# Denominator and gate products with 128 columns in place of 16 and 8

## The chip, the cores and the metric

The kernel runs on one core of one Trainium2 chip. The metric is the device time of one execution in microseconds (us); smaller is better. The engines are named as in the profile: PE is TensorE's matrix product, PEld its loading of weights, DVE is VectorE, ACT is ScalarE, POOL is GpSimd, SP issues DMAs.

## What is computed

The input is x of shape (16, 512, 128): 16 sequences of 512 tokens, all in float32. The reference does, with the constants 16 heads of width 8:

```python
x = x + linear_attention(layernorm(x), W_in, W_out)
    # q, k, v = projections; q, k clipped; Chebyshev polynomials T0..T10 of both
    # num = sum_p beta_p * Tq_p * cumsum(Tk_p * v)      over the sequence
    # den = sum_p beta_p * sum(Tq_p) * cumsum(sum(Tk_p))  per head and token
    # out = (num / (den + 1e-7)) @ W_out.T
x = x + ffn(layernorm(x))
    # h = x + causal softmax attention(layernorm(x)), 16 heads
    # logits = layernorm(h) @ gate_W + gate_b; top 2 of 8 experts, softmax of the two
    # h + sum over the two experts of w_e * (gelu(layernorm(h) @ W1_e + b1_e) @ W2_e + b2_e)
```

The changed lines belong to the denominator `den` (one value for each of 16 heads and each token) and to the logits (one value for each of 8 experts and each token).

## The kernel before

One sequence of 512 tokens is the unit of work and fills four tiles of 128 tokens (QT = 4). The 16 sequences go through a software pipeline. A pass of the loop works on up to six sequences at once, each in another stage: f (first normalisation and projections), h (linear attention), g (second projections), m (maxima of the scores), b (scores, exponentials and value products), t (second half of the block: output projection, normalisation, gate and dispatch to experts). The first passes have only the early stages and the last ones only the late stages. Within a pass every engine walks over 129 places, and a list written out by hand says at which place it does which step. TensorE keeps a fixed order: between the score products (line 1398 and 1401), the maxima (1372, 1374) and the value products (1418) it has `head_sums` at places 4 and 9, `turn_x2` at 25, `denominators` at 32, `gate` at 33, `turn_ln` at 43, `turn_rden` at 47, `project_q2` and `project_k2` (lines 1350 and 1353) at 51 and 52, `ranks` at 58, `output1` (line 1336) at 91. `output2` (line 1443) is at place 3.

Engines wait for each other by semaphores. `denominators` waits for VectorE's product `d_prod` and the running sums `kv_sum`; VectorE's `invert_den` waits for `den_mm` and reads 64 columns of X. `gate` waits for ScalarE's `h2_ready`; VectorE's `gate_top` waits for `gate_mm` and reads 32 columns of Z. X and Z are whole banks of PSUM, 512 float columns wide; `turn_rden` later writes X from column 128 to 255 on, and `ranks` later writes Z from column 0 on.

In a product `k.matmul(out, weights, moving)` the weights are loaded into the array and the moving operand streams through it. Float products appear in the profile as two instructions each, so four products are eight instructions. In both edited steps the tokens are the weights (128 by 128) and the small table moves: 16 columns of the constant table `cst`, or the 8 columns of the gate's weights `gw_sb`. The constant table goes on behind the 16 columns at `C_WS` = 128 with `C_SUM` at 144 and `C_SEL` at 208, and is 788 columns wide in the chip's memory.

After the passes the tokens are processed in 39 blocks by expert (lines 1561 and 1573). Just before, while the last sequences finish, `fold_bias` (line 1471) makes 32 products of one column, and the gate of the last sequence runs alone.

Of the kernel before, what the change touches and what calls it, by code (L numbers as in the profile page):

```python
# [26 lines left out]
P = 128  # L27
# [3 lines left out]
H, DH = 16, 8  # L31
E, HID = 8, 512
# [32 lines left out]
C_ID, C_WS, C_SUM, C_SEL, C_IO, C_RG, C_BN, C_TK, C_DU = 0, 128, 144, 208, 720, 728, 736, 776, 784  # L65
# [46 lines left out]
def block_kernel(nc, x, consts, cols, row_biases, w_in, w_out, wq, wk, wv, wp, gate_w, ew1, ew2, eb2, out):  # L112
    with ExitStack() as ctx:
        place = {}

        def sb(name, shape, dt=F32):
            tensor = ctx.enter_context(nc.sbuf_tensor(name, shape, dt))
            width = int(np.prod(shape[1:])) * (2 if dt == BF16 else 4)
            place[name] = nc.sbuf_base - -(-width // 32) * 32
            return tensor  # L120
# [10 lines left out]
        cst = sb("cst", [P, C_KEPT])  # L131
# [8 lines left out]
        gw_sb = sb("gw_sb", [P, E])  # L140
# [20 lines left out]
        ksum = sb("ksum", [P, T])  # L161
# [91 lines left out]
        h2 = lnT  # L253
        ident = cst[:, C_ID:C_ID + P]

        X, Y, Z, V = (ctx.enter_context(nc.psum_tensor(n, [P, T], F32)) for n in ("front0", "front1", "back0", "back1"))
# [989 lines left out]
        def _(pe):  # L1246
            k = nc.tensor
# [57 lines left out]
            def denominators(f):  # L1305
                pe.wait_ge(W.d_prod, f + 1)
                pe.wait_ge(W.kv_sum, f * ORDERS + 4)
                for t in range(QT):
                    last = k.matmul(X[:, t * H:(t + 1) * H], ksum[:, t * P:(t + 1) * P], cst[:, C_WS:C_WS + H],
                                    start=True, stop=True)  # L1310
                last.then_inc(W.den_mm, 1)

# [137 lines left out]
            def gate(b):  # L1450
                pe.wait_ge(W.h2_ready, b + 1)
                for t in range(QT):
                    last = k.matmul(Z[:, t * E:(t + 1) * E], h2[:, t * P:(t + 1) * P], gw_sb[:, :], start=True, stop=True)
                last.then_inc(W.gate_mm, 1)

            def ranks(t_):
# [18 lines left out]
            def body(t, b, m, g, h, f, p):  # L1475
# [3 lines left out]
                for n in range(SLOTS):  # L1479
# [15 lines left out]
                    if at(32, h):  # L1495
                        denominators(h)
                    if at(33, t):
                        gate(t)
# [123 lines left out]
```

## Time and profile before

| | us |
|---|---|
| Median of 3 runs without a profile | 1507.76 |
| Lowest and highest of them | 1507.52, 1512.24 |
| Profiled execution, device time | 1519.67 |
| Its span, first to last instruction | 1517.4 |
| Mean clock granted to TensorE, share of full | 0.903 |

The profiled execution is a run of its own: it is 11.9 us above the median of the others, and 2.3 us of its device time lie outside the span. Busy times count the instructions of an engine; products overlap, so that the duration of one holds part of the next.

### The profile page before, as it was taken

The numbers are of one execution on the slowest core, as the hardware profiler recorded it, in microseconds if no ns is written. First come the engines' busy times: TensorE is split into PE (matmuls) and PEld (weight loads), VectorE is DVE, ScalarE is ACT, GpSimd is POOL, SyncE is SP. The second block draws the span as 40 slices with busy tenths as digits, with TensorE's granted clock in tenths as the row PEclk, the third lists the DMA queues.
The fourth block names the chain that finished last, engine by engine and source line by source line (L and its number), as shares of the span: only waits on it lengthen the run. The fifth ranks groups of instructions, "written<-read, shape, count | busy, mean of one in ns | idle before, by whom it ended". The sixth has DMA issues, their size and how long they took to land.

```text
span 1517.4 us, 27667 instructions
## 1 busy us (share of the span) xinstructions
PE 1261.7 (83%) x8757; PEld 734.9 (48%) x8819; DVE 1153.8 (76%) x2622; ACT 910.5 (60%) x1795; POOL 848.8 (56%) x1077
## 2 busy tenths in 40 slices
PE   3465899999999989999999999988877399999870
PEld 1233354454544545445454454534335287888750
DVE  5658888999899888898888988845621588888754
ACT  1233476676766756666576676665462488888750
POOL 5776545667667676676756667430221246666570
PEclk8567799999999999999999999999895599999985
DMA  3032131422413224132241321431151212222128
GB/s 97 0 84 70 15 84 33 91 70 46 102 60 66 71 44 107 55 67 71 44 96 41 78 70 39 100 85 30 42 186 46 75 58 70 87 84 74 62 105 359
DMA packets 79344, 116.22 MB, mean 77 GB/s; under 512 B 15396, under 2 KB 61496, under 8 KB 74976
## 3 DMA queue, kind: packets, MB, share of 16 engines
q1 hardware_dynamic: 65888, 92.41, 23.4%
q0 software_dynamic: 9088, 17.33, 3.3%
q10 hardware_dynamic: 4224, 4.72, 0.9%
q8 instruction: 71, 1.16, 0.3%
q14 instruction: 73, 0.60, 0.1%
HBM read 58.29 MB, written 57.43 MB: 76 GB/s over the span
## 4 chain that ended last, share of the span: by engine, by line
PE 60%; DVE 17%; ACT 8%; issue 6%; DMA 3%; POOL 3%; another core or an unknown queue 1%; SPq 0%; DVEq 0%; POOLq 0%; ACTq 0%
PE back L1418 8%; PE scores L1398 8%; DVE nm L586 7%; PE maxima L1372 7%; PE front L1561 6%; PE back L1573 5%; PE front L1301 4%; PE maxima L1374 3%; DVE hn L460 3%; ACT pr L971 3%; PE front L1276 3%; PE back L1251 2%; PE scores L1401 2%; ACT rows L454 2%; DMA stack<-pairs 2%
## 5 line engine op out<-in xcount | busy, mean ns | idle before, releaser
L971 ACT ACTIVATE pr<-scores 128x384 f32<-128x384 f32 (+1 forms) x768 | 380.6, 524 | 223.7 <-PE scores L1401 189.7
L586 DVE TENSOR_REDUCE nm<-maxima 128x1 f32<-128x384 f32 (+3 forms) x704 | 426.3, 634 | 105.6 <-PE maxima L1374 86.7
L1398 PE MATMUL scores<-stack 98*128 98x512 bf16 (+3 forms) x1024 | 266.7, 310 | 41.4 <-ACT pr L971 35.1
L1372 PE MATMUL maxima<-stack 96*128 96x128 bf16 (+3 forms) x1024 | 256.7, 312 | 46.5 <-DVE nm L586 43.5
L1175 POOL DMA_INDIRECT xg<-rows,sloti x128 | 133.3, 1042 | 111.3 <-DVE sloti L656 71.5
L1398 PEld LDWEIGHTS scores<-stack 98*128 98x128 bf16 x1024 | 90.8, 100 | 210.4 <-ACT pr L971 135.0
L1401 PE MATMUL scores<-maskB,identb 128*128 128x128 bf16 (+1 forms) x768 | 186.5, 243 | 0.0
L1418 PE MATMUL back<-pr,vaug 128*9 128x512 f32 (+3 forms) x2048 | 183.1, 454 | 1.5 <-issue 1.5
L1372 PEld LDWEIGHTS maxima<-stack 96*128 96x128 bf16 x1024 | 89.9, 100 | 176.5 <-DVE nm L586 85.3
L1240 POOL DMA_INDIRECT pairs<-xs x104 | 106.7, 1026 | 92.6 <-DVE xs L821 60.8
L1374 PE MATMUL maxima<-maskA,identb 128*128 128x128 bf16 (+1 forms) x642 | 152.3, 237 | 0.0
L1561 PE MATMUL front<-h_first,w_now 128*128 128x512 f32 x312 | 128.7, 414 | 7.4 <-DVE h_second L801 3.3
L1110 ACT ACTIVATE xs<-front,b1p 128x512 f32<-128x512 f32 x156 | 107.2, 687 | 33.7 <-PE front L1561 23.8
L1145 POOL TENSOR_TENSOR kv<-F,kv 128x512 f32<-128x512 f32 x80 | 107.2, 1363 | 12.3 <-DVE kv L540 12.0
L1136 POOL TENSOR_SCALAR F<-F 128x512 f32<-128x512 f32 x32 | 56.7, 1771 | 72.4 <-DVE F L519 70.9
L1573 PE MATMUL back<-hid_first,w_now 128*128 128x512 f32 x312 | 97.1, 393 | 0.0
L540 DVE TENSOR_TENSOR_SCAN kv<-one,front 128x512 f32<-128x512 f32 x80 | 93.5, 1200 | 0.0
L814 DVE TENSOR_TENSOR hid_second<-xs,hid_first 128x512 fp32r<-128x512 f32 x99 | 68.0, 686 | 30.3 <-ACT hid_first L1091 24.7
L1156 POOL TENSOR_TENSOR kv<-kv 128x512 f32<-128x512 f32 x64 | 81.1, 1277 | 3.9 <-POOL kv L1156 0.4
L1401 PEld LDWEIGHTS scores<-maskB,identb 128*128 128x128 bf16 x768 | 76.5, 100 | 10.7 <-issue 4.0
L1161 POOL TENSOR_TENSOR xs<-xs,x2t 128x512 f32<-128x512 f32 x16 | 20.3, 1268 | 106.6 <-DVE x2t L608 84.7
L1091 ACT ACTIVATE hid_first<-xs 128x512 fp32r<-128x512 f32 x117 | 74.0, 633 | 3.7
(222 smaller groups left out, 2545.8 us busy)
## 6 DMA issues: line engine op xcount, KB each, us to landing
stack<-spread SPq DMA_DIRECT2D x64, 384.0 KB
spread<-qs SPq DMA_DIRECT2D x96, 128.0 KB
spread<-ks SPq DMA_DIRECT2D x96, 128.0 KB
xs<-xg SPq DMA_DIRECT2D x39, 272.0 KB
stack<-pairs SPq DMA_DIRECT2D x8, 1024.0 KB
xg<-xs SPq DMA_DIRECT2D x17, 272.0 KB
xs<-in_x SPq DMA_DIRECT2D x16, 256.0 KB
acc<-xs SPq DMA_DIRECT2D x16, 256.0 KB, 2.3
```

The source lines that it names most:

```text
L586: v.tensor_reduce(nm[:, h:h + heads, t], ring(n)[:, 0:heads * (t + 1) * P].rearrange("p (h n) -> p h n", h=heads), AX.X, ALU.max, negate=T ...
L971: a.activation(pr[:, n % PR, 0:width], ringE[n % 2][:, 0:width], ACT.Exp).then_inc(W.exp_ready, 1)
L1110: a.activation(gel[n % GS], (X, Y)[n % 2][:, :], ACT.Gelu, bias=b1p[:, bass.ds(ahead * HC + c, 1)]).then_inc(W.mid_ready, 1)
L1145: g_.tensor_tensor(kv[:, p, :], qx[p], kv[:, p, :], ALU.mult).then_inc(W.qk_prod, 1)
L1175: g_.indirect_dma_start(xg[:, :], bass.IndirectOffsetOnAxis(sloti[:, i, q:q + 1], 0), rows[:, i, q, :], None).then_inc(W.dispatched, 16)
L1372: k.matmul(ring(n)[:, at:at + (t + 1) * P], qst[p][0:MROW, h, t * P:(t + 1) * P], kst[p][0:MROW, h, 0:(t + 1) * P], start=(j == 0), stop=T ...
L1374: k.matmul(ring(n)[:, 0:heads * (t + 1) * P].rearrange("p (h n) -> p h n", h=heads)[:, :, t * P:(t + 1) * P], identb[:, :], maskA[:, 0:hea ...
L1398: k.matmul(dst[:, at:at + T - t * P], kst[p][0:MROW + 2, h, t * P:(t + 1) * P], qst[p][0:MROW + 2, h, t * P:T], start=(t == tiles[0]), sto ...
L1401: k.matmul(dst[:, 0:2 * P * many].rearrange("p (i n) -> p i n", i=many)[:, :, 0:P], identb[:, :], maskB[:, 0:many * P].rearrange("p (i n) ...
L1418: last = k.matmul(V[32 * i:32 * i + DH + 1, t * P:T], vaug[:, b % VR, t, 4 * (s_ // 3) + i, :], pr[:, (4 * s_ + i) % PR, at:at + T - t * P ...
L1561: last = k.matmul((X, Y)[n % 2][:, :], w_now[:, i % 2, wi, c * P:(c + 1) * P], h2p[hi][:, i % 2, :], start=(j == 0), stop=(j == len(TERMS3 ...
L1573: last = k.matmul((Z, V)[i % 2][:, :], w_now[:, i % 2, 2 + wi, c * P:(c + 1) * P], (hidh, hidl)[hi][i % 2 * HC + c], start=(c == 0 and j = ...
```

## The change

The four products of the denominators write 128 columns in place of 16, and their moving operand is 128 columns of the constant table from `C_WS` on. The output of each starts where it did, 16 columns after the last; what it writes behind its own 16 columns is overwritten by the next product or read by no one. The four products of the gate write 128 columns in place of 8; their moving operand is the gate's weights, repeated 16 times by a step of zero in its access pattern. The number of products, their order and all waits stay.

```diff
                 for t in range(QT):
-                    last = k.matmul(X[:, t * H:(t + 1) * H], ksum[:, t * P:(t + 1) * P], cst[:, C_WS:C_WS + H],
+                    last = k.matmul(X[:, t * H:t * H + P], ksum[:, t * P:(t + 1) * P], cst[:, C_WS:C_WS + P],
                                     start=True, stop=True)
                 last.then_inc(W.den_mm, 1)
...
                 for t in range(QT):
-                    last = k.matmul(Z[:, t * E:(t + 1) * E], h2[:, t * P:(t + 1) * P], gw_sb[:, :], start=True, stop=True)
+                    last = k.matmul(Z[:, t * E:t * E + P].rearrange("p (i n) -> p i n", n=E), h2[:, t * P:(t + 1) * P],
+                                    gw_sb[:, :].unsqueeze(1).to_broadcast((P, P // E, E)), start=True, stop=True)
                 last.then_inc(W.gate_mm, 1)
```

## Rows read from the trace of the kernel before

**Rows 1.** The page: busy us (share) xinstructions; granted clock by slice, in tenths.
```profile
PE 1261.7 (83%) x8757; PEld 734.9 (48%) x8819; DVE 1153.8 (76%) x2622; ACT 910.5 (60%) x1795; POOL 848.8 (56%) x1077
...
PEclk8567799999999999999999999999895599999985
```

**Rows 2.** The page: the chain that ended last, by engine.
```profile
PE 60%; DVE 17%; ACT 8%; issue 6%; DMA 3%; POOL 3%; another core or an unknown queue 1%; SPq 0%; DVEq 0%; POOLq 0%; ACTq 0%
```

**Rows 3.** Windows by pass: us, then busy (instructions) of each engine, clock, DMA.
```profile
433.00:494.60 61.60, 56.96 (x467) 30.49 (x470) 55.51 (x134) 41.85 (x90) 42.73 (x58) 1.00 0.29 71
...
556.30:619.70 63.40, 58.67 (x468) 31.00 (x470) 55.70 (x134) 41.86 (x90) 42.71 (x58) 0.97 0.30 68
...
619.70:684.40 64.70, 60.15 (x468) 31.24 (x470) 55.38 (x133) 41.89 (x90) 42.42 (x58) 0.95 0.28 68
...
878.40:941.40 63.00, 58.33 (x467) 30.92 (x470) 54.58 (x125) 41.84 (x90) 41.05 (x53) 0.97 0.27 65
```

**Rows 4.** Windows: stretches at and behind narrow products (618) and wide ones (1102).
```profile
618.00:621.10 3.10, 2.54 (x24) 1.80 (x20) 2.02 (x4) 2.36 (x5) 3.10 (x3) 1.00 0.02 5
...
621.40:624.50 3.10, 3.10 (x15) 0.81 (x16) 2.26 (x4) 0.49 (x1) 3.10 (x4) 0.50 0.00 0
...
1102.60:1105.80 3.20, 2.08 (x13) 1.35 (x14) 1.60 (x6) 1.59 (x4) 0.96 (x1) 1.00 1.13 350
...
1106.00:1109.00 3.00, 2.37 (x17) 0.62 (x16) 0.15 (x3) 2.03 (x6) 2.05 (x7) 1.00 1.13 333
```

**Rows 5.** Windows: stretches at and behind a wait, and the bias folding.
```profile
439.90:442.80 2.90, 1.29 (x14) 0.72 (x11) 2.69 (x18) 0.81 (x4) 1.86 (x2) 1.00 0.00 0
...
563.40:566.50 3.10, 1.29 (x11) 0.68 (x11) 2.89 (x18) 0.92 (x5) 1.74 (x2) 1.00 0.00 0
...
566.80:569.90 3.10, 3.10 (x4) 0.94 (x4) 1.60 (x9) 1.25 (x3) 0.00 (x0) 0.50 0.01 3
...
1153.00:1166.00 13.00, 13.00 (x63) 13.00 (x63) 0.00 (x0) 2.79 (x5) 0.00 (x0) 0.50 0.00 0
```

**Rows 6.** Timeline of TensorE at full clock: start us, us, operation, idle before.
```profile
433.04 1.01 PE L1309 MATMUL front<-cst,ksum 128*128 128x16 f32 x8
...
433.90 1.04 PE L1453 MATMUL back<-gw_sb,lnT 128*128 128x8 f32 x8
...
435.11 1.05 PE L1418 MATMUL back<-pr,vaug 128*9 128x512 f32 x8
...
586.07 1.05 PE L1336 MATMUL front<-wo_sb,outT 128*128 128x128 f32 x8
...
1102.80 1.16 PE L1443 MATMUL front<-wp_sb,hn 128*128 128x128 f32 x8 [0.62 <-ACT hn L979]
```

**Rows 7.** Timeline of TensorE: the query projection, and a pass with falls.
```profile
443.19 1.07 PE L1350 MATMUL front<-lnT,wq_sb 128*128 128x512 f32 x2
...
566.56 1.93 PE L1350 MATMUL front<-lnT,wq_sb 128*128 128x512 f32 x2
...
684.36 1.02 PE L1309 MATMUL front<-cst,ksum 128*128 128x16 f32 x8
...
686.64 1.90 PE L1418 MATMUL back<-pr,vaug 128*9 128x512 f32 x8
...
695.95 1.61 PE L1350 MATMUL front<-lnT,wq_sb 128*128 128x512 f32 x2
```

**Rows 8.** Groups by line of TensorE: busy us, mean ns, idle before and releaser.
```profile
L1309 PE MATMUL front<-cst,ksum 128*128 128x16 f32 x128 | 18.8, 281 | 22.0 <-DVE kv L540 22.0
...
L1453 PE MATMUL back<-gw_sb,lnT 128*128 128x8 f32 x128 | 17.5, 263 | 1.2 <-ACT lnT L983 1.2
...
L1443 PE MATMUL front<-wp_sb,hn 128*128 128x128 f32 x128 | 19.4, 297 | 0.6 <-ACT hn L979 0.6
```

**Rows 9.** Timeline of TensorE near the end: bias folding and a projection.
```profile
1152.69 13.65 PE L1471 MATMUL front<-col,stack 128*128 128x1 f32 x64
...
1166.20 2.05 PE L1443 MATMUL front<-wp_sb,hn 128*128 128x128 f32 x8
```

## The prediction

> **What bounds the kernel now.** I read the page's busy shares and slices first, then the chain that ended last, then the clock by stretch, and last the instructions around the two edited places. TensorE is the busiest engine and holds most of the chain [rows 1, 2]; in a steady pass of the pipelined loop it is busy 57.0 of 61.6 us, with VectorE close behind at 55.5 [rows 3]. So whatever slows TensorE in the middle of a pass lengthens the pass. What does slow it there is its own clock. The page's clock digits are high in the middle but the mean is 0.903, and passes differ in length though they hold the same instruction counts: four passes (310 to 556 us) granted 1.00 and took 61.5 to 61.9 us; one granted 0.97 and took 63.4; four granted 0.95 and took 64.6 to 64.7; one granted 0.97 and took 63.0 [rows 3], where one row stands for each kind of pass. VectorE, ScalarE and POOL do the same work in all of them. From this the price of a fall to the half clock (1.2 in place of 2.4 GHz) is 63.0 - 61.6 = 1.4 us for a first one in a pass, and 64.7 - 63.0 = 1.7 us for a second.
>
> Two places in the pass are followed by such a fall. The first is the pair of edited steps: the stretch that holds both narrow products is at 1.00, with TensorE counted busy 2.5 of 3.1 us, and the stretch right behind it is at 0.50 [rows 4]. That happens six times, near 249, 621, 686, 751, 816 and 881 us, in the twelve passes that hold the pair. The second place is the wait of TensorE for VectorE's normalisation and maxima, busy 1.3 of 3.1 us, after which the query projection starts at half clock [rows 5]. That happens five times from 556 us on. Neither is followed by a fall every time: the same pair and the same wait were passed at full clock in the four good passes. Where the chip takes its decision within the pass is not seen in any row; what is seen is that the falls come in runs once the pass has become longer.
>
> What was TensorE doing in the first place? Eight instructions of 16 columns, eight of 8, a few score products around them, and waits for ScalarE's exponentials between. The weights of each product are 128 by 128 floats and their loading sets the spacing: eight instructions (four products in two passes each) last 1.01 and 1.04 us, 0.11 us apiece, with hardly a column streamed [rows 6]. "Busy" is therefore not what keeps the clock: the plainest row is the bias folding near the end, 64 instructions of one column, back to back for 13.65 us, engine 100% busy, granted clock 0.50 throughout [rows 5, 9].
>
> **The change, part by part.** *Wider denominators and gate, direct cost.* The 128-column float products of the same kernel, with the same weight load, are the output projections: eight of them last 1.05 us at full clock [rows 6], mean 297 ns each against 281 and 263 for the two edited ones [rows 8]. So the pair costs 0.04 + 0.01 = 0.05 us more per pass, 16 passes, 0.8 us in all if none of it is covered. At half clock the narrow form takes 13.65 / 64 = 0.21 us each, while eight wide ones take 2.05 us with the tail of the last one [rows 9], against 8 x 0.21 and a like tail, 1.9 to 2.0: at most 0.1 us for each of the few early and late groups, inside the 0.8. VectorE reads the same columns as before, and no semaphore, wait, buffer or DMA is moved. In the first three passes TensorE starts the denominators only after a VectorE scan, 22.0 us of idle in all [rows 8], so there the cost is on the chain; it is the same 0.1 us.
>
> *The repeated gate weights.* No row shows a moving operand that is repeated by a zero step. Nearest is the wide projection with a plain operand, which gives nothing extra. The bound above is that each of the 128 instructions takes its duration twice over, 0.11 us more, 14 us. I take nothing: the operand still has runs of 8 floats and the column count is that of the plain one.
>
> The Trainium skill speaks against the cheap reading: "TensorE: Matmul & The Clock Gate", section "Back-to-back issue gap", gives about 60 cycles for up to 64 columns and 134 for 128. As an estimate from that page, 256 instructions x 74 cycles at 2.4 GHz are 7.9 us, and my sum would end near 1505 in place of 1497. The trace does not agree for float weights, 0.11 us for 8 or 16 columns as for 128 [rows 6].
>
> *What it gives back.* The pair now streams 128 columns sixteen times where it streamed 16 and 8. Wide products in the same spacing stand elsewhere in the pass, and no fall of the steady passes comes behind those. The best likeness is late in the kernel: a stretch with the eight wide instructions of an output projection and waits around them, TensorE busy only 2.1 of 3.2 us, less than at the pair, and the clock stays at 1.00 [rows 4, 6]. So I expect the six falls behind the pair to be gone: 6 x 1.4 = 8.4 us. Price seen directly: value products behind the pair take 1.90 us in place of 1.05 [rows 6, 7].
>
> *What is late next.* With the pair at full clock, the next place is the wait before the query projection. In the slow passes that projection begins 11.6 us after the first denominator product (695.95 - 684.36), in a good one 10.15 (443.19 - 433.04) [rows 6, 7]. In four of the five passes with a second fall the first had shifted it. In the undisturbed passes the wait was passed four times without a fall and once with one. From nothing to all of 4 x 1.7 = 6.8 us goes with the first falls; I take half, 3.4. If the single one at 567 us (63.4 - 61.6 = 1.8) goes as well the gain is at most 8.4 + 6.8 + 1.8 = 17.0.
>
> **Sum.** -8.4 - 3.4 + 0.8 = -11.0 us on the profiled execution, 1519.67 to 1508.7. That execution lies 11.9 us above the median of the runs without a profile, and nothing shows whether those runs had as many falls. The passes are the same work, so I carry the difference over: 1507.76 - 11.0, about 1497 us. This kernel's measurement tells a difference from about 0.3% on, here 4.5 us.
>
> **The rivals.**
> *Few falls in the runs timed.* If the 11.9 us between the profile and the median are falls that the plain runs don't have, only 5 us of the 17.0 are left to gain, and 2 to 5 us come: 1503 to 1506. For it: the three runs spread over 4.7 us, as a few falls more or less would. Against: the first 310 us and the end, which cannot tell a good pass from a bad one, may carry the difference just as well.
> *The clock does not look at columns.* Then nothing returns and 0.8 us is paid: 1508.6, no change. For it: during the pair the engine is counted busy 80% of the time and still falls, so what counts may be something this change doesn't touch; most of the added columns are zeros of the constant table. Against: the one-column products, and the 128-column projection at 65% busy without a fall [rows 4, 5].
> By the Trainium skill (same page, section "HAM oscillation") the clock is lost in gaps in which the engine waits; the pair leaves hardly any, and by that alone its widening would give nothing. The trace shows six falls behind the pair all the same [rows 4].
> *The fall moves.* If the pair's fall is only replaced by one at the wait behind it, in all ten passes in place of five, 5 x 1.7 = 8.5 us are added where 8.4 go, with the 0.8 about 1508.6, no change. Against: four good passes in a row.
> *Slower: the wide products take column time on top of the weight load, or the zero step makes the read slow.* Place: TensorE at the pair, where ScalarE's exponentials and VectorE's denominator wait. It decides from (11.0 + 4.5) / 256 = 0.06 us more per instruction; for the gate alone from 0.12. Adding a whole 128-column time of 0.11 to each of 256 gives +28 - 11, about 1525. Against: the output projections do both in 0.11.
>
> **How the numbers follow.** Forecast 0.68; few falls in the plain runs 0.10 (half of it beyond 0.3%); clock not by columns 0.09; fall moves 0.06; slower 0.07. Faster by over 0.3%: 0.68 + 0.05, and 0.01 for falls that move in part, 0.74; within 0.3%: 0.05 + 0.09 + 0.05 = 0.19; slower 0.07. The forecast's own range is 1490 (all 17.0 us and a little of the early passes) to 1503; the range given goes on to 1508, over the few-falls case and to the edge of no change, and leaves out slower and the worst of the unchanged.
>
> **What the profile of the changed kernel would show.** The two edited lines with 128 columns, means near 297 and at most 300 ns, eight in about 1.05 us. The stretch behind the pair at 1.00 in every steady pass, the value products there at 1.05 us. Passes of 61.6 us, at most one or two of 63.4, none of 64.7; mean clock from 0.903 to about 0.93. The same busy times on VectorE, ScalarE and POOL. I am wrong if a stretch behind a complete wide pair is at 0.50; if passes with a fall at the wait are as many as before; if the gate's instructions start more than 0.12 us apart; or if the falls are gone and the passes still take over 63 us, because VectorE at 55.5 of 61.6 holds them.

## The result and the profile after

The changed kernel takes 1514.68 us in the median of 10 runs, the kernel before 1507.72 in 10 runs beside it: a ratio of 1.0039 with a 95% interval of 1.0024 to 1.0055. It is slower by 0.4% where 0.7% faster was forecast. The profiled execution went the other way, 1516.34 us (span 1514.1) after 1519.67 before; the section on the prediction comes back to that.

The windows by pass of the changed kernel answer to [rows 3]. The columns are the stretch, its length, the busy time and instructions of PE, PEld, DVE, ACT and POOL, the granted clock, the DMA share and GB/s.

```profile
372.90:437.30 64.40, 59.04 (x471) 30.94 (x470) 56.56 (x134) 41.80 (x90) 42.37 (x58) 0.97 0.28 68
...
501.80:564.70 62.90, 57.53 (x471) 30.46 (x470) 56.51 (x133) 42.03 (x90) 42.36 (x58) 1.00 0.29 69
...
820.60:884.10 63.50, 59.06 (x471) 31.07 (x470) 54.75 (x133) 41.93 (x90) 42.74 (x58) 0.97 0.26 64
884.10:946.00 61.90, 57.46 (x472) 30.55 (x470) 54.75 (x125) 41.90 (x90) 41.40 (x53) 1.00 0.28 66
```

Two things are new. No pass has two falls of the clock any more. And a pass at full clock, the row at 501.80, takes 62.9 us in place of 61.6: PE's own busy time is only 0.6 us more than in [rows 3], but VectorE's has gone from 55.5 to 56.5.

The stretches around the pair, now wide (629.0, and the one behind it), and around the wait before the query projection:

```profile
629.00:632.20 3.20, 3.20 (x29) 2.12 (x28) 2.02 (x6) 1.19 (x3) 3.20 (x3) 1.00 0.02 5
632.40:635.50 3.10, 3.02 (x27) 1.74 (x29) 3.10 (x4) 2.17 (x5) 3.02 (x4) 1.00 0.00 0
636.80:640.20 3.40, 0.81 (x7) 0.39 (x7) 3.19 (x17) 0.79 (x4) 1.05 (x1) 1.00 0.00 0
640.60:643.60 3.00, 3.00 (x4) 0.96 (x4) 1.58 (x9) 1.22 (x3) 0.00 (x0) 0.50 0.00 0
```

Behind the pair the clock stays at 1.00, here and in all twelve passes that hold it, where [rows 4] had 0.50. It isn't that TensorE is counted busy for longer. The same stretch around the start of the denominators, of the kernel before (a fall came behind it) and of the changed one (none came):

```profile
617.97:621.17 3.20, 2.63 (x24) 1.90 (x20) 2.12 (x4) 2.39 (x5) 3.20 (x3) 1.00 0.02 5
```

```profile
627.30:630.50 3.20, 2.63 (x23) 1.89 (x20) 2.02 (x4) 2.40 (x5) 3.20 (x3) 1.00 0.02 5
```

But PE now works only 0.8 us of 3.4 before the query projection, against 1.3 of 3.1 in [rows 5], and the fall behind that wait comes in seven of the eleven passes from 245 us on (near 320, 384, 449, 576, 640, 705 and 832 us).

The reason for the longer wait is on VectorE. Its timeline in the pass from 501.77 us (the start of the denominators), with the duration behind the start:

```profile
502.92 0.23 DVE L560 TENSOR_SCALAR den<-front 128x64 f32<-128x64 f32 x1 [1.14 <-PE front L1309]
503.18 0.55 DVE L562 RECIPROCAL den<-den 128x64 f32<-128x64 f32 x1
503.65 1.09 DVE L586 TENSOR_REDUCE nm<-maxima 128x1 f32<-128x384 f32 x2
504.65 1.21 DVE L540 TENSOR_TENSOR_SCAN kv<-one,front 128x512 f32<-128x512 f32 x1
505.84 0.69 DVE L586 TENSOR_REDUCE nm<-maxima 128x1 f32<-128x512 f32 x1
506.44 4.27 DVE L460 TENSOR_SCALAR hn<-xs,mva,rstda 128x128 f32<-128x128 f32 x4
```

And that of the kernel before, in the pass from 433.04 us:

```profile
437.02 0.69 DVE L586 TENSOR_REDUCE nm<-maxima 128x1 f32<-128x512 f32 x1
437.63 3.16 DVE L460 TENSOR_SCALAR hn<-xs,mva,rstda 128x128 f32<-128x128 f32 x4
```

The same four instructions of the normalisation (`apply0`, line 460) take 4.27 us in place of 3.16, and they begin 506.44 - 501.77 = 4.67 us after the denominators in place of 4.59. The neighbour that matters is POOL. Its rows at the same moment, of the kernel before first, then of the changed one:

```profile
435.36 2.50 POOL L1156 TENSOR_TENSOR kv<-kv 128x512 f32<-128x512 f32 x2
437.81 1.28 POOL L1145 TENSOR_TENSOR kv<-F,kv 128x512 f32<-128x512 f32 x1
```

```profile
504.08 2.50 POOL L1156 TENSOR_TENSOR kv<-kv 128x512 f32<-128x512 f32 x2
506.54 1.27 POOL L1145 TENSOR_TENSOR kv<-F,kv 128x512 f32<-128x512 f32 x1
```

POOL changes from a sum (line 1156) to its next product (line 1145) at 437.81 and 506.54. VectorE's first normalisation instruction starts 0.18 us ahead of that change before, and lasts 0.34 us; after the edit it is 0.10 us ahead, and lasts 1.46 us, until POOL's whole next product is done. The remaining three take 2.8 us in both kernels. So a shift of 0.08 us makes VectorE wait for one product of POOL more, 1.2 us, in each of the nine passes from 245 to 821 us. In the last two passes POOL's change comes 0.3 us later and nothing is lost.

Last, TensorE's groups, to be read against [rows 8]:

```profile
L1309 PE MATMUL front<-cst,ksum 128*128 128x128 f32 x128 | 20.6, 311 | 22.0 <-DVE kv L540 22.0
...
L1453 PE MATMUL back<-gw_sb,lnT 128*128 128x128 f32 x128 | 18.1, 286 | 1.2 <-ACT lnT L983 1.2
```

### The profile page after: what moved, and what is told of

Its sections match the earlier page's. It is cut to its first block, busy times and chain, and to the rows that moved or that the text cites. A ratio compares the mean times of both kernels' runs of the same rounds, so it can differ in the third digit from the quotient of the medians.

```text
span 1514.1 us, 27729 instructions
## 1 busy us (share of the span) xinstructions
PE 1256.2 (83%) x8819; PEld 730.6 (48%) x8819; DVE 1162.2 (77%) x2622; ACT 911.8 (60%) x1795; POOL 849.7 (56%) x1077
## 4 chain that ended last, share of the span: by engine, by line
PE 61%; DVE 18%; ACT 8%; issue 6%; POOL 3%; DMA 3%; another core or an unknown queue 1%; SPq 0%; POOLq 0%; DVEq 0%; ACTq 0%
DVE nm L586 8%; PE scores L1398 7%; PE back L1418 7%; PE maxima L1372 7%; PE front L1562 7%; PE back L1574 6%; PE front L1301 4%; DVE hn L460 4%; ACT pr L971 3%; PE maxima L1374 3%; PE front L1276 3%; PE scores L1401 2%; PE back L1251 2%; ACT rows L454 2%; DMA stack<-pairs 2%
## 5 line engine op out<-in xcount | busy, mean ns | idle before, releaser
L1398 PE MATMUL scores<-stack 98*128 98x512 bf16 (+3 forms) x1024 | 263.5, 307 | 38.2 <-ACT pr L971 33.1
L1418 PE MATMUL back<-pr,vaug 128*9 128x512 f32 (+3 forms) x2048 | 176.7, 441 | 0.8 <-issue 0.8
L1374 PE MATMUL maxima<-maskA,identb 128*128 128x128 bf16 (+2 forms) x704 | 176.0, 250 | 0.0
```

The source lines that it names most:

```text
L1374: k.matmul(ring(n)[:, 0:heads * (t + 1) * P].rearrange("p (h n) -> p h n", h=heads)[:, :, t * P:(t + 1) * P], identb[:, :], maskA[:, 0:hea ...
L1398: k.matmul(dst[:, at:at + T - t * P], kst[p][0:MROW + 2, h, t * P:(t + 1) * P], qst[p][0:MROW + 2, h, t * P:T], start=(t == tiles[0]), sto ...
L1418: last = k.matmul(V[32 * i:32 * i + DH + 1, t * P:T], vaug[:, b % VR, t, 4 * (s_ // 3) + i, :], pr[:, (4 * s_ + i) % PR, at:at + T - t * P ...
```

## The experiments

Ten kernels ran. The first four were timed beside 29 runs of the kernel before, with a median of 1507.65 us. The other six ran on two other chips, beside 10 and 11 runs of the kernel before with medians of 1477.45 and 1477.56 us. Like passes at full clock took the same time on all three chips to 0.02 us (61.56), and the difference lies behind the last denominators, so ratios are compared from one chip to another, not times.

**Only the gate wide.**

```diff
-                    last = k.matmul(X[:, t * H:t * H + P], ksum[:, t * P:(t + 1) * P], cst[:, C_WS:C_WS + P],
+                    last = k.matmul(X[:, t * H:(t + 1) * H], ksum[:, t * P:(t + 1) * P], cst[:, C_WS:C_WS + H],
```

(Against the changed kernel.)

> Only the gate product is 128 columns wide; the denominators are 16 wide as before. Theory A (two effects: the wide pair keeps the clock, and the later end of the wide denominators makes VectorE miss its turn before POOL's next product, 1.2 us a pass): VectorE takes up the denominators 1.05 us after their start as before, the first instruction of its normalisation (line 460) lasts 0.34 us, full-clock passes take 61.6 us, and eight wide instructions are enough that no fall comes behind the pair; device time about 1500, some 0.5% under before. Theory B (whatever made the passes 1.2 us longer comes with any wide product, such as its reads of the chip's memory): full-clock passes take about 62.2 to 62.8 us, time 1508 to 1515. Theory C (eight wide instructions are too few for the clock): passes of 61.6 at full clock, but falls behind the pair stay, time about 1508 as before.

Measured: 1513.2 us, ratio 1.0032 (1.0017 to 1.0046), nearly that of the whole change. The slowness is here: VectorE's rows in the pass from 502.07 us are those of the changed kernel.

```profile
506.13 0.69 DVE L586 TENSOR_REDUCE nm<-maxima 128x1 f32<-128x512 f32 x1
506.74 4.24 DVE L460 TENSOR_SCALAR hn<-xs,mva,rstda 128x128 f32<-128x128 f32 x4
```

Again 4.67 us after the denominators, though these are narrow and VectorE took them up after 1.05 us. The route that theory A gave to the delay was wrong. No fall came behind the pair, so eight wide instructions are enough for the clock, and C falls.

**Only the denominators wide.**

```diff
-                    last = k.matmul(X[:, t * H:(t + 1) * H], ksum[:, t * P:(t + 1) * P], cst[:, C_WS:C_WS + H],
+                    last = k.matmul(X[:, t * H:t * H + P], ksum[:, t * P:(t + 1) * P], cst[:, C_WS:C_WS + P],
```

(Against the kernel before.)

> Only the denominators are 128 columns wide; the gate product is 8 wide as before. Theory A: VectorE takes up the denominators 1.14 us after their start, the first instruction of its normalisation lasts about 1.45 us, full-clock passes take 62.7 to 62.9 us; no fall behind the pair; device time 1512 to 1516, as with both. Theory B: half of the lengthening, passes of about 62.2 us, time near 1511. Theory C (eight wide ones too few): passes of 62.8 and falls behind the pair besides, 64 us, time near 1520.

Measured: 1493.34 us, ratio 0.9904 (0.9883 to 0.9925). All three theories missed the time: this half of the change, alone, gains 14.3 us, more than the 11 that had been forecast for the whole. A full-clock pass, and VectorE in the pass from 431.37 us:

```profile
369.80:431.40 61.60, 57.35 (x472) 30.51 (x470) 55.40 (x134) 41.89 (x90) 42.47 (x58) 1.00 0.29 71
```

```profile
432.51 0.23 DVE L560 TENSOR_SCALAR den<-front 128x64 f32<-128x64 f32 x1 [1.15 <-PE front L1309]
...
435.37 0.67 DVE L586 TENSOR_REDUCE nm<-maxima 128x1 f32<-128x512 f32 x1
435.95 3.16 DVE L460 TENSOR_SCALAR hn<-xs,mva,rstda 128x128 f32<-128x128 f32 x4
```

VectorE does take the denominators up 0.1 us later, but the start of the normalisation is 4.58 us: the scan and the maximum in between had that much slack. Ten of the eleven passes from 246 us on are at full clock, one falls at the wait.

Where, then, does the gate's width enter? VectorE's last maximum before the normalisation waits for TensorE's maxima. TensorE's rows of the kernel before (denominators at 433.04) and of the kernel with only the gate wide (502.07):

```profile
436.54 0.38 PE L1372 MATMUL maxima<-stack 96*128 96x512 bf16 x1
```

```profile
505.66 0.38 PE L1372 MATMUL maxima<-stack 96*128 96x512 bf16 x1
```

They start 3.50 and 3.59 us after the denominators; with only the denominators wide it is 3.50 again. The wide denominators are followed by the gate's products, each with a weight load of its own, and nothing behind them comes later; the wide gate is followed by scores, which come 0.09 us later. This reading, called A2, was put to the test by the next runs.

**The last denominator product narrow again, the rest wide.**

```diff
                 for t in range(QT):
-                    last = k.matmul(X[:, t * H:t * H + P], ksum[:, t * P:(t + 1) * P], cst[:, C_WS:C_WS + P],
+                    wide = H if t == QT - 1 else P
+                    last = k.matmul(X[:, t * H:t * H + wide], ksum[:, t * P:(t + 1) * P], cst[:, C_WS:C_WS + wide],
```

> Both products wide, but the last of the four denominator products 16 columns as before. Theory A: the end of the denominators comes 0.05 to 0.09 us earlier than with all four wide, VectorE's first normalisation instruction is back before POOL's turn (0.3 to 0.5 us in place of 1.45), full-clock passes 61.6 us, no fall behind the pair, time about 1500 to 1503. If the 0.03 us that the three others still add is too much, the first instruction stays at 1.45 us and the time near 1514. Theory B (any wide product costs): still 62.5 us a pass or more, time 1511 to 1514.

Measured: 1510.84 us, ratio 1.0028 (1.0006 to 1.0049), near that of the whole change. The end of the denominators is not the route, which runs over the gate. In four passes POOL stood later and VectorE got through; in one of them, that from 565.75 us, POOL was later by a hair only, and a timeline of VectorE and one of POOL show what that does:

```profile
570.42 1.54 DVE L460 TENSOR_SCALAR hn<-xs,mva,rstda 128x128 f32<-128x128 f32 x2
```

```profile
570.58 1.30 POOL L1145 TENSOR_TENSOR kv<-F,kv 128x512 f32<-128x512 f32 x1
```

VectorE began at 4.67 us after the denominators as in the other passes, but 0.16 us ahead of POOL's change, and got through: two instructions in 1.54 us in place of one in 1.44. That pass took 61.6 us. The outcome hangs on the two engines' order, not on the start by itself.

**One more VectorE instruction behind the reciprocal.**

```diff
+        spare = sb("spare", [P, 64])
...
                 v.reciprocal(den[:, :], den[:, :]).then_inc(W.den_rec, 1)
+                v.memset(spare[:, :], 0.0)
```

> The kernel before with one added VectorE instruction of 64 columns behind the reciprocal of the denominators; TensorE's work is unchanged. Theory A: the first instruction of the normalisation starts some 0.1 us later, misses POOL's change of instruction and lasts 1.2 to 1.45 us; full-clock passes take 62.7 to 62.9 us though no product is wider, and the falls behind the narrow pair stay; time 1515 to 1522. Theory B (the wide products themselves slow something): passes of 61.7 us, time 1508 to 1509.

Measured: 1510.02 us, ratio 1.0009 (0.9985 to 1.0033). As a test of a later start it failed: the instruction fell into the slack just described, and in undisturbed passes the normalisation still began at 4.59. But its trace tells two things all the same. In the pass from 371.05 us VectorE was on time and POOL 0.24 us earlier than usual:

```profile
375.64 4.11 DVE L461 TENSOR_SCALAR hn<-xs,mva,rstda 128x128 f32<-128x128 f32 x4
```

```profile
375.58 1.26 POOL L1147 TENSOR_TENSOR kv<-F,kv 128x512 f32<-128x512 f32 x1
```

VectorE came 0.06 us behind POOL's change, its first instruction took 1.29 us, the query projection began 11.2 us after the denominators, and the clock fell at that wait. No product is wide in this kernel, so the loss needs none, which speaks against B. And with the narrow pair the clock fell behind it in seven of the twelve passes (near 249, 437, 563, 689, 754, 816 and 942 us).

**The last gate product narrow, the rest wide.**

```diff
                 for t in range(QT):
-                    last = k.matmul(Z[:, t * E:t * E + P].rearrange("p (i n) -> p i n", n=E), h2[:, t * P:(t + 1) * P],
-                                    gw_sb[:, :].unsqueeze(1).to_broadcast((P, P // E, E)), start=True, stop=True)
+                    wide = E if t == QT - 1 else P
+                    last = k.matmul(Z[:, t * E:t * E + wide].rearrange("p (i n) -> p i n", n=E), h2[:, t * P:(t + 1) * P],
+                                    gw_sb[:, :].unsqueeze(1).to_broadcast((P, wide // E, E)), start=True, stop=True)
```

> Denominators wide, and three of the four gate products wide, the last 8 columns. Theory A2 (the wide gate product that stands last pushes TensorE's following scores and maxima back by 0.09 us; VectorE's last maximum before the normalisation comes that much later, 4.67 in place of 4.59 us after the denominators' start, and misses the change between two POOL products): with the last one narrow the start is 4.59 or 4.60 again, the first normalisation instruction 0.34 us, passes 61.6 us, time 1491 to 1496 as with only the denominators wide. Theory B2 (the gate's operand repeated by a zero step is what costs): passes of 62.4 to 62.8 us, time 1507 to 1514.

Measured: ratio 0.9893 (0.9867 to 0.9918). Seven of the eight wide products, six of eight instructions of the gate repeated by a zero step, and the slowness is gone. In the pass from 432.08 us:

```profile
436.67 3.16 DVE L460 TENSOR_SCALAR hn<-xs,mva,rstda 128x128 f32<-128x128 f32 x4
```

```profile
434.38 2.50 POOL L1156 TENSOR_TENSOR kv<-kv 128x512 f32<-128x512 f32 x2
436.84 1.29 POOL L1145 TENSOR_TENSOR kv<-F,kv 128x512 f32<-128x512 f32 x1
```

VectorE is 0.17 us ahead of POOL's change again. B2 is refuted.

**One narrow gate product more, nothing else wide but the denominators.** Against the kernel with only the denominators wide:

```diff
-                for t in range(QT):
+                for t in (0, 0, 1, 2, 3):
                     last = k.matmul(Z[:, t * E:(t + 1) * E], h2[:, t * P:(t + 1) * P], gw_sb[:, :], start=True, stop=True)
```

> Denominators wide, gate 8 columns wide, and the first gate product made twice with the same result: no wide or repeated operand at the gate, only 0.22 us more of TensorE. Theory A2: the normalisation starts 0.22 us later, 4.8 us after the denominators' start, behind POOL's change, its first instruction waits for a whole POOL product (about 1.3 us), the query projection begins 11.3 us after in place of 10.15, full-clock passes take 62.7 to 63 us; falls come back at the longer wait; time 1505 to 1514. Theory B2: passes of 61.8 us, time 1495 to 1497.

Measured: ratio 1.0069 (1.0046 to 1.0092), by the ratios 1.7% above the kernel with only the denominators wide, for 16 x 0.22 = 3.5 us of added TensorE work. From the fifth denominators to the last its profile has 700.6 us, against 679.9 there. VectorE and POOL, pass from 502.33 us:

```profile
507.13 4.12 DVE L460 TENSOR_SCALAR hn<-xs,mva,rstda 128x128 f32<-128x128 f32 x4
```

```profile
504.64 2.49 POOL L1156 TENSOR_TENSOR kv<-kv 128x512 f32<-128x512 f32 x2
507.10 1.27 POOL L1145 TENSOR_TENSOR kv<-F,kv 128x512 f32<-128x512 f32 x1
```

Now VectorE comes 0.03 us behind POOL's change and waits 1.31 us for its first instruction. Full-clock passes take 62.75 to 62.9 us (61.8 in the last, where POOL stood later), and seven of eleven passes fall at the longer wait, as many as in the changed kernel. A delay that comes from narrow products does at this place what the wide gate did.

**The changed kernel with POOL's products cut to 4 columns.**

```diff
-                    g_.tensor_tensor(kv[:, p, :], qx[p], kv[:, p, :], ALU.mult).then_inc(W.qk_prod, 1)
+                    g_.tensor_tensor(kv[:, p, 0:4], qx[p][:, 0:4], kv[:, p, 0:4], ALU.mult).then_inc(W.qk_prod, 1)
...
-                    g_.tensor_tensor(kv[:, o, :], kv[:, a, :], kv[:, c, :], ALU.add).then_inc(W.n_add, 1)
+                    g_.tensor_tensor(kv[:, o, 0:4], kv[:, a, 0:4], kv[:, c, 0:4], ALU.add).then_inc(W.n_add, 1)
```

> The changed kernel with POOL's products and sums of the linear attention cut to 4 of 512 columns (the numerators are left unfinished); their semaphores are the same. If it is POOL's instructions that hold up VectorE's normalisation: its four instructions take 0.33 us or less each, 0.6 to 1.0 us together in place of 4.26, though the gate is wide and they start at 4.67 us, and the passes are 60 us or less. If VectorE is slowed by something else, such as TensorE's reads: still 3 to 4.3 us together.

Measured: one run, 1422.01 us; a pass takes 59.8 us at full clock.

```profile
410.93 0.69 DVE L586 TENSOR_REDUCE nm<-maxima 128x1 f32<-128x512 f32 x1
411.54 1.10 DVE L460 TENSOR_SCALAR hn<-xs,mva,rstda 128x128 f32<-128x128 f32 x4
```

Four instructions in 1.10 us in place of 4.27, 0.34 each with overlap, a little above the expected sum. So it is POOL's full-width instructions that VectorE's normalisation waits for. The clock did not fall in any of these passes.

**The gate's step moved behind the maxima.** Against the changed kernel, both products wide.

```diff
                     if at(32, h):
                         denominators(h)
-                    if at(33, t):
+                    if at(39, t):
                         gate(t)
```

> The changed kernel, both products wide, with TensorE's gate step moved from place 33 to 39 of the pass, behind the maxima that VectorE reduces before its normalisation. Theory A2: the maxima come 0.9 us earlier, VectorE starts the normalisation at about 3.7 to 4.0 us after the denominators' start, waits for POOL's change at 4.8 and gets it, so that the second instruction starts at 4.84 as in the fast passes; full-clock passes 61.6 us or a little less; no or one fall; ratio to the kernel before about 0.989. If the gate, now alone among the scores, delays them so that the following maximum or the projection comes later, passes of 62 us or more and a ratio near 1.

Measured: 1462.42 us, ratio 0.9891 (0.9866 to 0.9916). The passes and the ratio are as expected, the start of the normalisation is not: 4.58 us, because VectorE was busy with the scan until then and cannot come earlier than that. TensorE's maxima now begin 2.7 us after the denominators, so the 0.09 us no longer reach VectorE. The change as given, with the gate six places later, gains 1.1% where 0.7% had been forecast for it.

**Bias folding wide as well.** Against the kernel with only the denominators wide:

```diff
-                    last = k.matmul(X[:, n:n + 1], w1_sb[:, n // HC, n % HC * P:(n % HC + 1) * P], col[:, V_B2:V_B2 + 1],
+                    last = k.matmul(X[:, n:n + P], w1_sb[:, n // HC, n % HC * P:(n % HC + 1) * P], col[:, V_B2:V_B2 + 1].to_broadcast((P, P)),
                                     start=True, stop=True)
```

> Denominators wide, gate narrow, and the 32 one-column products of the bias folding near the end made 128 columns wide with the column repeated; each next product overwrites what is behind its own column. By the clock part of theory A, columns keep or bring back the clock: the folding begins at 0.50 and goes to 1.00 after a few us, the 64 instructions take 8 to 10 us in place of 13.2 to 13.7, the output projection behind it 1.1 in place of 2.05; as the folding is on the chain that ends last, 3 to 6 us less than with only the denominators wide, 1488 to 1490. If columns of a repeated operand don't count for the clock: still 13.5 us at 0.50, time about 1493.

Measured: 1456.38 us, ratio 0.9852 (0.9826 to 0.9878). The timeline row of the folding, and a window in it:

```profile
1109.91 7.31 PE L1471 MATMUL front<-col,stack 128*128 128x128 f32 x64
```

```profile
1110.00:1113.00 3.00, 3.00 (x29) 3.00 (x28) 0.00 (x0) 2.85 (x5) 0.00 (x0) 1.00 0.03 9
```

The narrow folding, in the kernel with only the denominators wide, took 13.31 us. The clock fell 0.4 us after its start and stayed down; its window:

```profile
1136.00:1145.00 9.00, 9.00 (x43) 9.00 (x44) 0.00 (x0) 0.00 (x0) 0.00 (x0) 0.50 0.00 0
```

The wide one kept the full clock throughout, better than expected. In the kernel with only the denominators wide the clock had been at half shortly before as well (1119 to 1129 us), which the wide run had not. The kernel with the gate at place 39 leaves that out: its clock was at 1.00 from 816 us on until 1.5 us into the narrow folding, and then at 0.50 for all the rest of it:

```profile
1111.22 12.29 PE L1472 MATMUL front<-col,stack 128*128 128x1 f32 x64
```

TensorE is 100% busy in all of them, and the repeated operand keeps the clock as a plain one does.

**Both:** the kernel with the gate at place 39 and the folding wide.

> The same with the bias folding 128 columns wide besides. By theory A2 and the measured 6 us of the wide folding the ratio is about 0.985, like that of the run with wide denominators and wide folding; the folding takes 7.3 us in place of 13.3.

Measured: 1456.15 us, ratio 0.9852 (0.9825 to 0.988). The folding takes 7.31 us, as expected. The kernel without it, timed on the same chip, took 1462.42, so the 64 wide instructions are worth 6.3 us. This and the run before it are the fastest of the full kernels; they can't be told apart.

## Why the prediction was wrong

*Falls behind the pair: right.* Six before and seven in the other kernel with a narrow pair; none in the changed kernel or in the nine others with a wide product at this place. The folding shows the same thing by itself. The price was near: the last of these passes took 63.0 us with a fall and 61.8 without one, 1.2 us, where the prediction took 1.4; it had compared that pass with fuller ones (POOL had 53 instructions there and 58 in them, VectorE 125 and 134), as if they did the same work. The rival in which the clock does not look at columns, and the estimate from gaps alone, fall.

*What is late next: right in direction, wrong in outcome.* A fall at the wait does go with the falls behind the pair when nothing else changes: with only the denominators wide one of eleven passes has it, against five before. In the changed kernel it came in seven, since the wait itself had grown, and the same seven of eleven came when a narrow product made the wait grow. That falls at the wait would be no fewer than before was one of the prediction's own signs of being wrong.

*The step that failed is the direct cost*: "So the pair costs 0.04 + 0.01 = 0.05 us more per pass, 16 passes, 0.8 us in all if none of it is covered". On TensorE it was 0.09 us at the maxima in place of 0.05, and all of it from the gate, for which the sum had 0.01. What was missing is what is queued on it: maxima, VectorE's last maximum, VectorE's normalisation, and POOL's next product, whose start VectorE had been beating by 0.18 us. The delay is multiplied there from 0.09 to 1.2 us a pass. The prediction had no term for it: "no semaphore, wait, buffer or DMA is moved" is true of the code, but VectorE's busy time went from 55.5 to 56.5 us a pass, where the same had been forecast. With the prediction's prices for a fall and the 1.2 us measured: -6 x 1.4 for the falls that went, +9 x 1.2 for the passes in which VectorE missed the turn (the sum had +0.8), +2 x 1.7 for two more falls at the wait (the sum had -3.4), +5.8 us in place of -11.0. The passes from the start of the fifth denominators to the last took 700.5 us in the changed kernel's profile and 694.5 in that of before (941.4 - 246.9): +6.0. With only the denominators wide the same stretch took 679.9.

```profile
245.50:946.00 700.50, 643.15 (x5162) 339.50 (x5160) 617.99 (x1455) 461.00 (x980) 466.43 (x622) 0.98 0.28 67
```

```profile
246.30:926.20 679.90, 632.36 (x5161) 335.49 (x5160) 607.03 (x1456) 460.49 (x980) 466.69 (x622) 1.00 0.29 69
```

*Few falls in the runs timed: it does not hold.* All 29 timed runs of the kernel before have a lower mean clock (0.899 to 0.918) than any of the six with only the denominators wide (0.921 to 0.923), and between these two kernels the medians moved by 14.3 us where the passes of the two profiles moved by 14.6. So the timed runs had falls too, and these numbers speak for about as many as in the profile. The profiled execution of before lay 11.9 us above the median. Its passes do not explain that: outside the stretch above it spent 822.9 us, the changed kernel 813.6, the one with only the denominators wide 808.6. So it was slow elsewhere than in the passes (5 us of it between the last denominators and the bias folding: 211.3 us, against 205.9 in the changed kernel), and slower than any of the 29 runs (1495.4 to 1519.46). This also is why the two profiled executions compare the other way round than the medians.

*The repeated gate weights: nothing, as taken.* The wide gate's instructions have a mean of 286 ns, 23 more than the narrow ones and less than the plain wide projection's 297 [rows 8]; the denominators, with a plain operand, went from 281 to 311, above the 300 that the prediction gave as the most. The Trainium skill's price of more columns, 7.9 us in all by the prediction's estimate, was not paid at the denominators. At the gate, where scores follow and not float weights, 0.09 us a group was, where that estimate gives 8 x 0.03 = 0.25, and it decided.

*The rival on the slower side* had the right place (TensorE at the pair, VectorE waiting) and the wrong mechanism: it had VectorE wait for its denominator and asked for 0.06 us per instruction; VectorE waited for its maximum, and 0.09 per group of eight sufficed.

The behaviour between the two engines is stated in the Trainium skill, "SBUF — State Buffer", section "SBUF: two separate sides": VectorE in some of its modes and POOL share a pair of ports, which whoever starts first holds for the whole instruction. The traces agree that VectorE waits for POOL's whole instruction: from the fifth denominators on, in all kernels with POOL's full width, its first instruction takes 0.34 us where it starts 0.16 to 0.20 us ahead of POOL's next product, and 1.29 to 1.46 where it starts 0.07 to 0.10 ahead of it or 0.03 to 0.06 behind. They don't agree on who counts as the first: by its recorded start VectorE was first at 0.10 us ahead too, and lost. No run shows whether its instruction is in one of those modes.

What stays open: from what lead on VectorE gets its turn. Ahead of a product of POOL that follows a sum it lies between 0.10 and 0.16 us. Ahead of a sum that follows a product 0.11 us was enough, in the changed kernel's first sequence:

```profile
39.93 3.96 DVE L460 TENSOR_SCALAR hn<-xs,mva,rstda 128x128 f32<-128x128 f32 x4
```

```profile
40.05 2.54 POOL L1156 TENSOR_TENSOR kv<-kv 128x512 f32<-128x512 f32 x2
```

Its first instruction took 0.32 us there; why the two differ is not shown. Open is also why POOL stands 0.3 us later in the last two of these passes, so that the loss does not come. It does so in the kernel with only the denominators wide too, so the wide gate isn't the cause.

## What to carry to other kernels

Products with few columns kept TensorE busy here without always keeping its clock; where each product has its own weight load, more columns, even useless ones, cost next to nothing and kept it at 1.00. Look what starts behind the last of them: put the widened step where another with its own weight load follows, or behind what another engine waits for. And where VectorE and POOL alternate, measure the lead that one has over the other's next instruction; a delay that eats up part of the lead (0.08 of 0.18 us here) can cost a whole instruction of the other.

## What the runs showed of the hardware

The distance between gain and loss was 0.08 us a pass out of 61.6. Sixty-four loads of 128 x 128 float weights with one column each ran at 0.21 us apiece at the half clock, 13.31 us; with 128 columns each at 0.11 us at full clock, 7.31 us: more work in little over half the time. The spread of the timed runs was smaller without the falls: 1495.4 to 1519.5 us in 29 runs before, 1490.8 to 1494.6 in 6 with the denominators wide.
